# Ten expert tiles and the tile plan become steps of the written attention order

## The reference, cut to what matters

```python
# 32 items of 112 rows, width 256; context of 375 rows per item
x = x + tanh(g_xattn) * cross_attention(layernorm(x), ctx, ctx)     # 16 heads of 16
y = layernorm(x)
a = _ln(y + self_attention(y), ln1_g, ln1_b)                        # 16 heads of 16, per item
gates = softmax(a @ gW + gb)                                        # 8 experts
top2_scores, top2_idx = top_k(gates, 2)
h = relu(einsum('nd,edf->enf', a, W1) + b1)                         # 256 -> 512
ff = einsum('ne,end->nd', w_top2, einsum('enf,efd->end', h, W2) + b2)
x = x + tanh(g_ffn) * _ln(a + ff, ln2_g, ln2_b)
```

## Time and profile before

| what | value |
|---|---|
| runs | 1093.43, 1088.21, 1091.28 us, median 1091.28 |
| the profiled execution | 1092.1 us, its span 1090.4 us, mean granted clock 0.983 |
| busy in the span | PE 1032.9, PEld 846.6, DVE 827.3, ACT 700.3, POOL 281.1 us |
| chain that ended last, by engine | PE 22%, DVE 4%, issue 3%, POOL 1%, DMA 1% |

### The profile page before, as it was taken

One profiled execution on the slowest core, in us unless ns is written; L12 is line 12 of the kernel. 1 busy time (PEld: TensorE's weight loads), 2 busy tenths in 40 slices (PEclk: granted clock), 3 DMA queues, 4 the chain that ended last, 5 costly groups with the idle time before them and its releaser, 6 DMA issues. The chain is left out here.

```text
span 1090.4 us, 35973 instructions
## 1 busy us (share of the span) xinstructions
PE 1032.9 (95%) x13328; PEld 846.6 (78%) x13328; DVE 827.3 (76%) x2334; ACT 700.3 (64%) x1337; POOL 281.1 (26%) x396
## 2 busy tenths in 40 slices
PE   7999999999999999999999999999965999999992
PEld 5777878777787877888777787777744999999992
DVE  7666667688888878888787887887885667777775
ACT  5776767777777777777777777777642334344341
POOL 1011111213222232222212141312432223444434
PEclk9999999999999999999999999999996999999997
DMA  3332132312111111211110021100213524343432
GB/s 108 110 97 76 41 99 68 92 60 74 42 46 43 42 46 46 56 38 38 37 56 28 25 58 47 40 22 27 70 32 92 173 88 122 122 125 123 122 120 97
DMA packets 53579, 77.69 MB, mean 71 GB/s; under 512 B 10561, under 2 KB 37569, under 8 KB 53281
## 3 DMA queue, kind: packets, MB, share of 16 engines
q1 hardware_dynamic: 43392, 52.39, 17.0%
q0 software_dynamic: 6096, 15.66, 4.3%
q10 hardware_dynamic: 3920, 7.34, 2.1%
HBM read 51.32 MB, written 24.05 MB: 69 GB/s over the span
## 5 line engine op out<-in xcount | busy, mean ns | idle before, releaser
L852 ACT ACTIVATE probs<-quad 125x1792 f32<-125x1792 f32 (+1 forms) x128 | 213.3, 1666 | 21.2 <-PE quad L1432 21.0
L930 ACT ACTIVATE scored_half<-quad 112x500 bf16<-112x500 f32 (+1 forms) x256 | 132.6, 574 | 56.1 <-PE quad L1420 55.9
L1123 DVE TENSOR_REDUCE part_max<-quad 112x8 f32<-112x1000 f32 x96 | 114.8, 1196 | 46.0 <-PE quad L1420 45.7
L959 ACT ACTIVATE tile_w<-hidden_w 128x1024 f32 x63 | 66.5, 1055 | 110.5 <-PE quad L1616 102.4
L1616 PE MATMUL quad<-tile_inT,tile_w 128*128 128x128 f32 x1008 | 124.6, 277 | 0.0
L1628 PE MATMUL quad<-output_w,hiddenT 128*128 x504 | 119.3, 380 | 0.6 <-DVE hiddenT L1339 0.6
L1616 PEld LDWEIGHTS quad<-tile_inT,tile_w 128*128 128x128 f32 x1008 | 119.4, 194 | 0.1
L747 POOL TENSOR_TENSOR inv_std_N<-moments_N,minus_half 112x1 f32<-112x1 f32 x32 | 17.6, 548 | 374.1 <-DVE moments_N L1031 374.1
L1126 DVE TENSOR_REDUCE part_max<-scored_half 112x8 f32<-112x1000 bf16 x96 | 113.6, 1184 | 0.0
L1420 PE MATMUL quad<-kT_A,qT_A 32*112 32x125 f32 (+2 forms) x1536 | 106.4, 390 | 0.7 <-DVE r L1226 0.4
L800 POOL DMA_INDIRECT kept_dram<-tile_out,take_back x63 | 62.4, 991 | 157.8 <-DVE tile_out L1360 144.5
(11 more groups left out here) (234 smaller groups left out, 1983.1 us busy)
## 6 DMA issues: line engine op xcount, KB each, us to landing
ctxT<-in_ctxT_dram SPq DMA_DIRECT2D x32, 375.0 KB, 3.3
tile_in<-sent_dram SPq DMA_DIRECT2D x63, 129.0 KB, 2.2
join_in<-kept_dram SPq DMA_DIRECT2D x14, 512.0 KB, 3.7
hidden_w<-in_hidden_w_dram SPq DMA_DIRECT2D x8, 512.0 KB, 4.5
output_w<-in_output_w_dram SPq DMA_DIRECT2D x8, 512.0 KB
x_in<-in_x_dram SPq DMA_DIRECT2D x32, 112.0 KB
x_res<-in_x_dram SPq DMA_DIRECT2D x32, 112.0 KB, 2.0
x_dram<-x_shift SPq DMA_DIRECT2D x32, 112.0 KB, 1.9
```

The lines of the kernel that those rows point to most:

```text
L852: act.activation(probs[0:rows, t.buffer("probs", step), :, :], bank_of(t, step)[0:rows, :, 0:U * T], ACT.Exp, scale=SCALE).then_inc(taken[ ...
L930: act.activation(scored_half[:, t.buffer("half", step), i * n:(i + 1) * n], bank[0:T, RT // 2 + i, 0:n], ACT.Copy).then_inc(copied[kind], 1)
L1123: dve.tensor_reduce(part_max[:, 0:RT // 2, f:f + RT], bank[0:T, 0:RT // 2, 0:KEYS].rearrange("t r (j s) -> t r j s", s=SC), AX_X, ALU.max) ...
```

## The change

1. `LAST` is a new list, with thirteen new steps: `P.early` and `P.first` (a plan of the first ten tiles from the rows of the first eleven items), ten of each of `T.load`, `T.w`, `T.x`, `T.h`, `T.y` (one tile's load, weight copy, transposes, hidden product and output product with what DVE and POOL do behind it), and `P.keys`, `P.rank`, `P.table`, `P.spread` (the old plan, cut in four). `FIRST` is changed in some places and `ORDER` runs ten times instead of eleven.
2. `EXPERTS` starts at tile 10. The bodies of its stages are now functions that steps and loop share.
3. The plan sorts the ten tiles that are done to the front (`early`, `is_early`).
4. `LATEST` of the first three chunks is 22, 25, 27 (was 12, 15, 19), and `READY` spaces the chunks: 22, 25, 27, 29, 31, 33, 35, 40, then as before; it was 12, 15, 19, 24, 27, 31, 34, 40.
5. The steps' products and copies take attention's banks, one at a time, in place of the fixed banks of the loop.

```diff
-BEGIN, END = 14, 25
+BEGIN, END = 14, 24
+EARLY, KNOWN = 10, 10
-EXPERTS = Plan(NT, NT, TR, {"A": 0, "B": 1, "D": 2}, ["A.x", "B.hT", "D.y"], {})
+EXPERTS = Plan(NT, NT, TR, {"A": 0, "B": 1, "D": 2}, ["A.x", "B.hT", "D.y"], {}, EARLY)
 LAST = """
...
+    E.gate T.load E.oN T.y E.copy T.y E.pick E.aT T.x T.w T.load E.out T.x T.w T.h T.w E.rank T.h E.send E.norm T.x
+    T.y E.gate T.h E.pick T.x T.y E.send E.rank T.h T.load E.send P.keys T.y P.rank E.copy T.y P.table P.spread""".split()
-LATEST = [min(NT, (TOP * T * -(-(n + 1) * JW * P // T) + E * (P - 1)) // P) - 1 for n in range(JT)]
+BEFORE = [-(-(n + 1) * JW * P // T) for n in range(JT)]
+LATEST = [min(NT, (TOP * T * k + E * (P - 1)) // P + (0 if k > KNOWN else EARLY)) - 1 for k in BEFORE]
+for n in reversed(range(JT - 1)):
+    LATEST[n] = min(LATEST[n], LATEST[n + 1])
+READY = LATEST[:]
+for n in range(1, JT - 2):
+    READY[n] = max(READY[n], READY[n - 1] + 2)
 def chunks(turn, ahead):
-    return [n for n in range(JT) if LATEST[n] + ahead == turn]
+    return [n for n in range(JT) if READY[n] + ahead == turn]
@@ SP
+            def fetch(n, first):
+                if n >= TR:
+                    sp.wait_ge(tile_done, n - TR + 1)
+                sp.dma_start(tile_in[:, n % TR, :], io["sent"][bass.ds(first, P), :]).then_inc(tile_loaded[n % TR], DMA)
-                    elif step == "B.pv" and t.item("B") == NB - 1:
-                        keys_over(sp)
-                        sp.dma_start(output_b[:, :], ...)
+                    elif step == "T.load":
+                        n = t.item("T")
+                        if n == 0:
+                            keys_over(sp)
+                            sp.dma_start(output_b[:, :], ...)
+                            sp.wait_ge(taken["P.first"], 1)
+                            for k in range(2):
+                                sp.wait_ge(sent[k], (KNOWN + 2 - k) // 2 * DMA * TOP)
+                        fetch(n, sp.value_load(first_table[0:1, n + EARLY:n + EARLY + 1], min_val=0, max_val=E * REGION - P))
@@ POOL
+                    elif step == "T.y":
+                        keep(t.item("T"))
+            def keep(n):
+                k = n % 2
+                pool.wait_ge(taken_back, n + 1)
+                pool.wait_ge(tile_done, n + 1)
+                settled(pool, passed_pool)
+                pool.indirect_dma_start(out=io["kept"], ..., in_=tile_out[:, k, :], in_offset=None).then_inc(out_stored[k], DMA)
@@ ACT
+            def bring(n, e):
+                if n >= 2:
+                    act.wait_ge(ex_made["B.hT"], n - 1)
+                act.activation(tile_w[:, n % 2, :, :], hidden_w[:, :, bass.ds(e * F, F)], ACT.Copy).then_inc(weights_moved, 1)
@@ DVE
+            def hidden_out(n, e, bank):
+                dve.wait_ge(ex_made["B.hT"], n + 1)
+                if n >= 2:
+                    dve.wait_ge(ex_made["D.y"], n - 1)
+                for f in range(FC):
+                    ins = dve.tensor_scalar(hiddenT[:, n % 2, f, :], bank[:, f * P:(f + 1) * P],
+                                            hidden_b[:, f, bass.ds(e, 1)], 0.0, ALU.add, ALU.max)
+                ins.then_inc(ex_taken["B.hT"], 1)
+                    elif step == "P.early":
+                        dve.memset(ones_f[:, :], 1.0).then_inc(early_steps, 1)
...
+                        dve.tensor_tensor(known[:, :], history[:, KNOWN + 1, :], region_of[:, :], ALU.subtract).then_inc(early_steps, 1)
...
+                    elif step == "T.h":
...
+                        expert_of[n] = dve.value_load(first_table[0:1, n:n + 1], min_val=0, max_val=E - 1)
+                        hidden_out(n, expert_of[n], bank)
+                    elif step == "T.y":
...
+                        output_out(n, expert_of[n], bank)
+                        planned(17)
+                        dve.tensor_tensor(is_early[:, :], tile_row[:, :], tile_early[:, :], ALU.is_lt).then_inc(plan_steps, 1)
+                        planned(18)
+                        dve.scalar_tensor_tensor(key_bias[:, :], is_early[:, :], float(-2 * NB * P), key_bias[:, :], ALU.mult,
+                                                 ALU.add).then_inc(plan_steps, 1)
@@ PE
+                    elif step == "T.h":
+                        hidden(t.item("T"), bank)
```

More of the change, by code:

```diff
@@ L78, in run @@
     def run(self, eng, do):
-        for b in range(self.peeled):
+        for b in range(self.first, self.peeled):
             do(Turn(self, b))
@@ L108, in __init__ @@
             self.add(s, done)
-        assert all(n == (1 if s[0] in once else items) for s, n in done.items())
+        assert all(n == times(s) for s, n in done.items())
         self.starts = {}
@@ L141, in places @@
                 holds[k] = use
[L142 removed]
+        return banks, freed, holds
     def run(self, eng, do):
@@ L236 @@
 LAST = """
[L237 to L241, removed]
@@ new lines @@
+    C.qk0 E.norm A.v0 E.out C.qk1 E.rank C.bias N.ctx E.send E.copy F.aT B.s2 M.mT A.v1 F.out X.max D.s A.v0 E.gate
+    C.v F.load E.aT C.yT A.k1 C.bias A.q F.res E.pick E.send C.qk0 E.norm P.early E.rank C.qk1 X.mT E.gate M.max0
+    F.res D.pv B.pv F.norm X.max F.res D.s F.oN E.oN E.out A.v1 F.aT F.shift E.send E.aT N.ln M.max1 B.s0 A.k0 C.v
+    A.xT B.s1 X.mT E.norm E.pick A.q E.out D.s C.yT E.rank F.load F.out F.shift D.pv C.bias F.load M.max2 B.s2 C.qk0
+    A.k1 C.qk1 E.gate E.oN F.norm M.mT T.load E.copy M.max0 B.pv E.pick E.copy X.max B.s0 F.oN C.yT C.v C.bias
@@ new lines @@
+    E.norm E.aT M.max1 B.s1 E.send F.aT E.rank F.res E.send D.pv E.copy M.max2 B.s2 E.out C.qk0 E.oN M.mT E.gate
+    B.pv T.load E.pick E.send C.bias B.s0 E.rank C.v T.load F.oN E.aT F.out P.first F.norm E.norm B.s1 F.aT T.load
+    X.mT A.v0 C.qk1 E.gate B.s2 E.out F.shift F.out A.v1 C.yT X.max D.s B.pv F.shift F.norm E.pick X.mT E.rank C.qk0
+    E.copy F.oN D.s F.aT C.qk1 E.norm E.gate C.v E.pick D.pv D.pv E.rank E.oN T.w T.load F.out C.yT E.oN F.res E.aT
+    X.max T.x E.copy C.bias C.qk0 T.w T.load E.out T.h C.qk1 X.mT F.norm C.v E.send T.w T.x E.aT E.norm X.max
@@ L448, in build @@
         result = sb("result", [P, JR, JW, D])
-        in_psum = [k for k in ATTENTION.repeats if k != "E.gate" and k.split(".")[1] not in
-                   ("load", "ln", "norm", "pick", "send", "shift", "bias", "res", "set", "mask", "copy", "ctx", "K", "Q", "V", "B", "R", "C")]
+        in_psum = [k for k in ATTENTION.repeats if k != "E.gate" and k[0] != "T" and k.split(".")[1] not in
+                   ("load", "ln", "norm", "pick", "send", "shift", "bias", "res", "set", "mask", "copy", "ctx", "K", "Q", "V", "B", "R", "C", "early", "keys")]
         made = {k: sem("made_" + k.replace(".", "_")) for k in in_psum}
@@ L586, in join_rest @@
         def join_rest(steps):
-            for turn in range(EXPERTS.turns, LATEST[-1] + STORE + 1):
+            for turn in range(EXPERTS.turns, READY[-1] + STORE + 1):
                 steps(turn)
@@ L1633, in _ @@
+                if t.active("D"):
+                    n = t.item("D")
+                    e = pe.value_load(table[0:1, n:n + 1], min_val=0, max_val=E - 1)
+                    if n < EARLY + 2:
+                        bank_left(pe, 4 + n % 2)
+                    else:
+                        pe.wait_ge(ex_taken["D.y"], n - 1)
+                    output(n, e, output_bank[n % 2])
             EXPERTS.run(pe, expert_turn)
```

502 lines of the change are left out of this document (287 added, 215 removed).

## The result

The change takes 1085.38 us (median of 20 runs, 1080.25 to 1087.25); the kernel before, run beside it, 1092.05 (20 runs, 1086.66 to 1094.80). The ratio is 0.9941 with a 95% interval of 0.9928 to 0.9953: 6.7 us faster, where 1086 was forecast.

The account below looks back on a forecast made before the run. PE bounds both sides of a 23.3 us hole where DVE's chains set the pace. DVE's 25.5 us sum puts tile 11 11.8 us earlier; less 6.0 for ten s, 5.8 us off 1092.1: 1086, range 1077 to 1096.

Parts of the forecast that it names:

- The yardstick: Start of tile 11's hidden product, 875.09 us before; what it comes earlier is the gain, unless the joins take it back.
- Last values to `table`: From the last item's weighted values of cross-attention to `table`: 25.5 us more on DVE, plus 6.0 for ten times s.
- The register read: DVE's load of the expert number starting each `T.h`, 0.30 and 0.19 us; bounded between 0.2 and 0.5 us a tile.
- s: Time each of the ten early tiles holds DVE up beyond 2.58 us: taken as 0.6 us, bounds 0.2 and 1.2.
- DVE over 90%: Sign in the new profile: DVE busy over 90% from the last weighted values to `table`.
- DVE's side, which is longer: Sum of DVE's added time before `table`, 25.5 us, against PE reaching the last ranks 17 us later.
- The moved steps at 1.4 us: Behind the last weighted values: one more pick, rank, norm and second norm, one pair of row maxima less; 1.4 us more.
- PE's side: 773.3 to 823.3 us: some 32 us of tile work against 15.4 idle, so PE reaches the last ranks 17 us later.
- the full hole: Rival: between attention and experts the hole fills completely, PE's clock stays at 2.4 GHz; gain 12.4 us, 1079; chance 0.18.
- The plan: Tile plan between attention and experts: about three links more at 0.2 us, two fewer at its head; + 0.4 us.
- The joins: Seven chunks every two turns in the loop: 6.8 us of DVE work in 7.47, costing nothing; losing rival's chance 0.05.
- the worst case: In the joins, POOL contention slows DVE: 9.2 us against 7.47 per two turns, seven chunks costing 12 us.

Follow-up runs that it names:

- x2: The change with DVE's ten early tile steps taking expert 0 as a constant instead of the register read: 1078.76 us, ratio 0.9878 to the kernel before.
- x6: The change with DVE reading the next tile's expert number right behind the current tile's `hiddenT` instructions: 1080.96 us, ratio 0.9906 to the kernel before.
- x3: The change with one more DVE instruction of 0.42 us, result unused, in each early tile's output: 1086.55 us, ratio 0.9953 to the kernel before.
- x4: The change with four more PE transposes, results unused, in each early tile: 1086.41 us, ratio 0.9945 to the kernel before.
- x1: The kernel before with the change's `FIRST` and `LAST` order but none of the thirteen new steps: 1099.66 us, ratio 1.0071 to the kernel before.
- x5: The change with tile 9's output step moved from before `P.table` to behind `P.spread`: 1080.94 us, ratio 0.9912 to the kernel before.
- x9: The change with the tile steps between the last item's output product and its rank, and two inside the plan, moved behind the rank: 1088.72 us, ratio 0.9981.

## Why the prediction was right, and where its steps were not

- **The time.** 1086 forecast, 1085.38 measured. The yardstick moved 5.0 us (875.09 to 870.05) for a forecast of 5.8. It is made up of 6.6 us counted from the last values, less 1.6 us by which the part before came later in this profile; other profiles with that part in the same order lie up to 5 us earlier. Behind the last product another 1.2 us came, for which the prediction had no term. So the gain came from where it was forecast, between the last values and tile 11, but that the time came out within 1 us is in part luck.
- **Last values to `table`.** 57.6 + 25.5 + 6 = 89.1 forecast, 88.6 measured; `table` at 861.06 us for 860. From `table` to tile 11 9.0 us for 9.28, the first tile at half clock in 3.41 us, as forecast. The prediction's signs also name a stretch of "about 80 us" instead of 55, which doesn't follow from its own sum (55.1 + 31.5 = 86.6); measured the same way it is 86.1.
- **The register read.** Named as nearly the whole of s, bounded at 0.2 to 0.5 us a tile. x2 shows 0.5 us a tile, the upper end. The gaps ahead of `hiddenT`, read and wait together, are 6.5 us or 0.65 a tile, where s was 0.6. The other part, DVE's wait for its own hidden product, can't be read from the change alone, since the read hides it; with the reads moved (x6) it is 0.9 us in three places.
- **DVE over 90%.** Wrong. It is 84% and PE 93% up to the rank, 83% and 87% up to `table` (PE's over 85% holds). The step that failed is "DVE's side, which is longer": up to the rank PE's busy time grew by 34.7 us and DVE's by 19.1, and PE came out as the fuller engine. By x3 and x4 neither sets the pace alone. DVE's sum held all the same, because it counted the gaps too: from the last values to `table` DVE's busy time grew by 23.2 us (50.03 to 73.24) and its idle time by 7.8: 6.5 came ahead of `hiddenT` and 1.6 ahead of tile 9's output, the 1.8 for sent rows went, and the rest is small gaps.
- **The moved steps at 1.4 us.** Wrong in its part: x1 has 9.7 us for the new order by itself, and then a tile costs 2.1 us and not 2.58 + s. The two errors cancel in the total, and that is luck. DVE's work was not what was missing (x1 has no more of it than the kernel before); the order's own waits were put at nothing. I had read the old order's holes as the ones the tiles would fill; they fill holes that the new order makes for them. `FIRST` at zero within 2 us holds (x1's last values 0.7 us later).
- **PE's side.** 17 us later was the floor if no idle time were left. PE still idles 5.4 us up to the rank, and the rank comes 24.7 us later.
- **Hole and clock.** The clock fell at the plan as forecast, so the full hole did not come. It was also forecast that ten `hiddenT` groups would have idle time of 0.2 to 0.5 us for PE. Nine have idle time, of 0.48 to 1.17 us, and the read is in it; six of the nine are not put down to PE at all.
- **The plan.** Priced at 0.4 us for links; it grew from 5.3 to 11.6 us. Up to `keys` it has 2.2 us more (3.05 to 5.24), mostly tile 9's hidden rows with their read (849.65 to 851.4 us); behind `keys` 4.1 more, with two tiles' outputs (2 x 1.4) and a half-clock product that DVE waits 1.63 us for. The tiles' work is in the 25.8 us of the sum; the 1.63 us were in no term, and x5 takes them out.
- **The joins.** Nothing: PE is full from 875 to 1055 us (180.00 of 180.00), and the change's `take_back` and `tile_raw` there have the means of before. `join_gain` takes 478 ns in either kernel, so the 12 us of the worst case did not come. The Trainium skill, "GPSIMD Engine Reference", section "Specifications", says that GpSimd shares its SBUF interfaces with VectorE and that VectorE's instructions with two SBUF inputs contend. The row of 1.07 us in attention agrees; these means show nothing of it. The worst case also counted seven chunks two turns apart, and `READY` has five such gaps.

Means in 876 to 1055 us of the change, and under them before (x48 and x20 in both):

```profile
L1141 DVE SCALAR_TENSOR_TENSOR take_back<-tile_in,row_is_new,spill_to 128x1 uint32<-128x1 f32 x48 | 12.1, 252 | 20.0 <-PE quad L1592 19.4 <-DMA kept_dram<-tile_out,take_back 0.7
L1146 DVE SCALAR_TENSOR_TENSOR tile_raw<-tile_sum,tile_in 128x256 f32<-128x256 f32 x48 | 24.2, 503 | 1.7
```

```profile
L1351 DVE SCALAR_TENSOR_TENSOR take_back<-tile_in,row_is_new,spill_to 128x1 uint32<-128x1 f32 x48 | 11.9, 247 | 19.1 <-PE quad L1628 19.1
L1356 DVE SCALAR_TENSOR_TENSOR tile_raw<-tile_sum,tile_in 128x256 f32<-128x256 f32 x48 | 24.2, 505 | 1.7
```

What stays open: why x1's order is 9.7 us longer link by link, 0.8 of the 2.6 us between x2 and x6, and the 1 us behind the last product.

## What to carry to other kernels

Work that fills holes in a hand-written order can be priced by its busy time on the fuller engines, but the order around it is part of the price: run the order without the work too, or the two terms can't be told apart. Look at what a step does on the sequencer: "issue" idle time ahead of an instruction on a chain between two engines can be on the path nearly in full (4.9 us for ten reads here), and moving it behind a long instruction gave back half of that. Look for the gap that it opens there. When steps are placed inside a serial plan, ask of each whether the plan's result waits for it.

## What the runs showed of the hardware

- A DVE register read from SBUF takes 0.30 + 0.19 us on the sequencer. Where it stood ahead of `hiddenT`, DVE was idle for 0.48 to 1.17 us in nine of ten cases, and ten of them cost 4.9 us (x2). Moved behind a group of 1.13 us, the timeline names no idle time in seven of nine cases and 0.4 us in two (x6).
- PE's granted clock was 0.55 from 855 to 860 us, close to its level of 1.2 GHz, while tile 9's output product took 3.77 us instead of the later 1.73; PE had idled 4.5 us for `keys` just before. With the tile steps in one block behind the rank (x9) it fell as well, to 0.80 over 28.1 us.
- Adding 3.7 us of PE work to a stretch where PE was 93% busy made it 1.3 us longer (x4).
